# Norms and FFN of a finished half spread over 13 and 9 steps, slot scores as one stacked float32r pass, its set-up moved into the first attention

## The reference

```python
x = x + attn_a(layernorm(x))        # 16 heads of 128, causal softmax attention
x = x + ffn(layernorm(x))           # int8 quantised rows @ int8 weight, scaled, + bias, as float16
x = x + attn_b(layernorm(x))        # 16 heads, rope, 64 slots per head, gated
x = x + ffn(layernorm(x))

# ffn: q = round(x / scale), scale = max|x| per row / 127; out = (q @ w.T) * scale * w_scale + bias
# attn_b, the slot scores and what hangs on them:
s   = clip(hs @ Ws1.T @ Ws2.T + bs2, -32, 32)     # Ws1: 256 -> 16, Ws2: 16 -> 16 heads * 64 slots
z   = cumlogsumexp(s, over time); es = exp(s); enz = exp(-z)
A   = tril(rope(q) @ rope(k).T * scale)
qv  = softmax(enz * (A @ es)); W2 = tril((qv * enz) @ es.T); o = W2 @ v
out = (rmsnorm(o) * g_w * silu(g)) @ Wo.T
```

## The kernel before

| r | what |
|---|---|
| 1 | `sum_rows` (PE), `add_rows`, `ln_stats` (DVE) |
| 2 | `ln_rsqrt` (POOL), `ln_scale`, `ffn_quant` (DVE) |
| 3 | `ffn_transpose` (PE), `ffn_copy` (ACT) |
| 4 | `ffn_product` (PE), `ffn_out` (DVE), `ffn_add` (POOL) |
| 5 | `ffn_add`, `ln_rsqrt` (POOL), `ln_stats` (DVE) |
| 6, 7 | `ln_scale`, `tail` (DVE), `transpose_x` (PE), `transposed` (ACT) |
| 8 | `s1_product` (PE), `s1_copy` (ACT) |

## Time and profile before

### The profile page before, as it was taken

How to read it: one execution, slowest core, us unless ns; L and a number is a source line. 1 busy time by engine, 2 the same in 40 slices (tenths; PEclk the granted TensorE clock), 3 DMA queues, 4 the chain that set the end, 5 groups by cost and what they waited for, 6 DMA issues and landing times.

```text
span 836.5 us, 13230 instructions
## 1 busy us (share of the span) xinstructions
PE 775.7 (93%) x4550; PEld 658.7 (79%) x4550; DVE 595.8 (71%) x1510; ACT 475.2 (57%) x1261; POOL 375.0 (45%) x356
## 2 busy tenths in 40 slices
PE   7999999998989998977897999999996999999973
PEld 6878888887878886866776888888885878888862
DVE  5545555567764457878797888888887788888855
ACT  4656656655565665644545666665663556666520
POOL 5243223223332243552645656665572665666411
PEclk9999999999999999988999999999999999999997
DMA  8211111121111221110101101111210111110100
GB/s 258 78 51 51 62 53 51 56 84 44 50 50 59 78 63 39 39 50 13 52 13 51 50 28 56 58 42 35 63 52 13 52 39 39 62 53 13 38 1 25
DMA packets 43283, 43.22 MB, mean 52 GB/s; under 512 B 3521, under 2 KB 42945, under 8 KB 43090
## 3 DMA queue, kind: packets, MB, share of 16 engines
q1 hardware_dynamic: 43218, 42.38, 16.0%
HBM read 41.33 MB, written 1.05 MB: 51 GB/s over the span
## 4 chain that ended last, share of the span: by engine, by line
PE 80%; DVE 11%; ACT 4%; issue 2%; POOL 2%; DMA 1%; SPq 0%; POOLq 0%; DVEq 0%; ACTq 0%
PE ps L1454 19%; PE ps L1643 10%; PE ps L1530 6%; PE ps L1461 5%; PE ps L1487 4%; PE ps L1657 3%; PE ps L1535 3%; PE ps L1512 3%; PE ps L1495 2%; PE ps L1684 2%; PE ps L1704 2%; PE ps L1723 2%; PE ps L1705 2%; PE ps L1670 2%; PE ps L1658 2%
## 5 line engine op out<-in xcount | busy, mean ns | idle before, releaser
L403 POOL TENSOR_TENSOR w_lo<-w_raw,w_hi 128x512 fp32r<-128x512 f32 x64 | 82.0, 1293 | 85.4 <-ACT w_hi L599 84.5
L1454 PE MATMUL ps<-xT_hi,w_hi 128*128 128x512 f32 x256 | 110.0, 430 | 4.2 <-ACT rot_s L747 2.3
L1149 DVE TENSOR_TENSOR wt<-ps,const 128x384 f32<-128x384 f32 x128 | 68.1, 553 | 47.2 <-PE ps L1658 27.3
L1454 PE MATMUL ps<-xT_hi,w_lo 128*128 128x512 f32 x256 | 101.4, 396 | 0.0
L1454 PE MATMUL ps<-xT_lo,w_hi 128*128 128x512 f32 x256 | 101.2, 395 | 0.0
L471 POOL TENSOR_TENSOR rot_s<-rot_s,const 128x512 f32<-128x512 f32 x64 | 81.4, 1282 | 20.4 <-ACT rot_s L747 20.4
L659 ACT ACTIVATE wt<-wt,negmax 128x128 f32<-128x128 f32 (+1 forms) x128 | 56.7, 444 | 21.9 <-DVE negmax L1044 21.8
L403 POOL TENSOR_TENSOR wc_lo<-wv,wc_hi 128x512 fp32r<-128x512 f32 x16 | 20.4, 1274 | 100.1 <-ACT wc_hi L599 100.1
L1032 DVE TENSOR_TENSOR v<-ps,bv_b 128x256 f32<-128x256 f32 x64 | 26.9, 422 | 50.7 <-PE ps L1461 50.7
L493 POOL TENSOR_TENSOR qp<-oke,enz 128x256 f32<-128x256 f32 x32 | 23.7, 739 | 83.4 <-ACT oke L771 83.4
L1137 DVE RECIPROCAL enz<-zs 128x128 f32<-128x128 f32 x64 | 60.3, 942 | 0.0
(11 more groups left out here) (159 smaller groups left out, 2354.6 us busy)
## 6 DMA issues: line engine op xcount, KB each, us to landing
w_raw<-a_w_q SPq DMA_DIRECT2D x16, 256.0 KB, 3.1
w_raw<-a_w_k SPq DMA_DIRECT2D x16, 256.0 KB, 3.8
...
```

Source lines behind the costliest of these rows:

```text
L403: g.tensor_tensor(lo[:, :, :], raw[:, :, :], hi[:, :, :].bitcast(F32), ALU.subtract).then_inc(ph.w_lo, 1)
L1149: d.tensor_tensor(dst, src[:, 0:384], tri3, ALU.mult).then_inc(done, 1)
L1454: ins = mm(PJ[bank], w[:, m, c, h * P:(h + 1) * P], x[:, c, cols], start=(t == 0), stop=(t == len(terms) - 1))
```

## The change

The extra work of a half is now written once, as `portion(f, half, r)` with `f` = 0 for the FFN between the attentions and `f` = 1 for closing, and fills `r` = 1 to 13 (`f` = 0) or 1 to 9 (`f` = 1):

| r | PE | DVE | ACT | POOL |
|---|---|---|---|---|
| 1 | `sum_rows` x2 | `add_rows` x2 | | |
| 2 | | `ln_stats` x2 | | |
| 3 | | | | `norm_half`: scale, 4 tiles of `xn` |
| 4 | | `ffn_range`, 4 tiles in one reduce | | |
| 5 | | | | `clear_sums` (`f` = 0) |
| 6 | | `ffn_round` x2 | | |
| 7 | `ffn_transpose` x2 | | `ffn_copy` x2 | |
| 8, 9 | `ffn_product` | | `ffn_scaled` | `ffn_tail` |
| 10 | | `ln_stats` x2 | | |
| 11 | | | | `norm_half` |
| 12, 13 | `transpose_x` | | `transposed` | `x_tail` |
| 13 | `s1_product` x2 | `s1_tail` x2 | `s1_copy` x2 | |

Rows 10 to 13 are for `f` = 0 alone. The tail of the program keeps its old form. Normalising, the two last operations of the FFN's output and `xT_lo` have gone from DVE to POOL, the scaling by the row scale from DVE to ACT.

The slot scores: `ws1` now has 96 columns with `Ws1` three times (at 0, 32 and 64), `ws2` three copies of `Ws2` and two of the bias, and ACT and DVE leave in `s1` the high part in rows 0 to 63 and the low part in rows 64 to 95. One float32r matmul over all 128 rows then gives hi*hi + hi*lo + lo*hi. The loads and zeroing for this stand in steps 0 to 8 of attention a and no longer at the start. The sums `accT` are cleared in step 1 and no longer in step 2. In even b steps ACT copies the turned slot weights (`slot_copy`) ahead of task "c3", and DVE clips ahead of the gate.

```diff
-        ws1 = sb("ws1", [P, C, RANK])
-        s1 = sb("s1", [P, B * T])
-        ws2 = sb("ws2", [P, HEADS * M])
+        ws1 = sb("ws1", [P, C, STACK])
+        s1 = sb("s1", [P, B * T], F32R)
+        ws2_s = sb("ws2_s", [P, HEADS * M], F32R)
+        one_rows = sb("one_rows", [P, 1])
         rot = sb("rot", [P, 2, HALF])
+        ws2 = rot[:, :, :].rearrange("p k t -> p (k t)")
...
# SP, in the loop over phases of attention a
+                if phase == 3:
+                    sp.wait_ge(init_done, 4)
+                    for o in (0, 32, 64):
+                        sp.dma_start(ws1[:, :, o:o + RANK], b_ws1.rearrange("(c p) n -> p c n", p=P)).then_inc(slot_ld, 16)
+                        sp.dma_start(ws2[o:o + RANK, :], b_ws2).then_inc(slot_ld, 16)
...
# POOL
+            def norm_half(k, half):
+
+                n, four = norms[k], slice(4 * half, 4 * half + 4)
+                pool.wait_ge(n.mv, 4 * half + 4)
+                g.tensor_scalar(var8[:, four], mv[:, four, 1], LN_EPS, None, ALU.add).then_inc(n.eps, 1)
+                pool.wait_ge(n.eps, half + 1)
+                g.tensor_tensor(rstd[:, four], var8[:, four], minus_half[:, four], ALU.pow).then_inc(n.rstd, 1)
+                pool.wait_ge(n.rstd, half + 1)
+                for t in range(4 * half, 4 * half + 4):
+                    g.tensor_scalar(xn[:, t, :], acc[:, t, :], mv[:, t, 0:1], rstd[:, t:t + 1],
+                                    ALU.subtract, ALU.mult).then_inc(n.xn, 1)
+
+            def ffn_tail(f, b):
+
+                F, two = ffns[f], slice(2 * (b % 2), 2 * (b % 2) + 2)
+                pool.wait_ge(F.y, b + 1)
+                g.tensor_tensor(y32[:, :, :], y32[:, :, :], ws_b[:, :].unsqueeze(1).to_broadcast([P, 2, D]), ALU.mult).then_inc(F.yw, 1)
+                pool.wait_ge(F.yw, b + 1)
...
+                g.tensor_tensor(y16[:, two, :], y32[:, :, :], fb_b[:, :].unsqueeze(1).to_broadcast([P, 2, D]), ALU.add).then_inc(F.y16, 1)
+                ffn_add(f, b)
+
+            def x_tail(b):
+
+                cols = slice(b * T, (b + 1) * T)
+                pool.wait_ge(xts[1].hi, b + 1)
+                g.tensor_tensor(xT_lo[:, :, cols], xT[:, :, cols], xT_hi[:, :, cols].bitcast(F32), ALU.subtract).then_inc(xts[1].lo, 1)
...
-                if x == 2:
+                if x == 1:
                     clear_sums(None, 0)
                     clear_sums(None, 1)
...
# POOL, b_step: even and odd steps
                         rope_mul(ahead, "q1", 0, 1)
+                    portion(0, 1, x)
+                    portion(1, 0, x - PHASES)
                     if nxt:
                         slots(x + 1)
...
                         rope_mul(ahead, "k1", 1, 1)
+                    portion(0, 1, x)
+                    portion(1, 0, x - PHASES)
                     rms(x)
...
# ACT
-                s.activation(s1[0:RANK, b * T:(b + 1) * T], ps[0:RANK, 7, o:o + T], ACT.Copy).then_inc(s1_done, 1)
+                s.activation(s1[0:STACK, b * T:(b + 1) * T], ps[0:STACK, 7, o:o + T], ACT.Identity,
+                             bias=one_rows[0:STACK, 0:1]).then_inc(s1_hi, 1)
+            def ffn_scaled(f, b):
...
+                for t in range(2):
+                    ins = s.activation(y32[:, t, :], ps[:, 7, t * D:(t + 1) * D], ACT.Copy, scale=qsc[:, 2 * b + t:2 * b + t + 1])
+                ins.then_inc(F.y, 1)
...
                 if x % 2 == 0:
+                    slot_copy(x)
                     b_task(phase, "c3")
-                    slot_copy(x)
...
# DVE
+            def s1_tail(b):
+
+                cols, o = slice(b * T, (b + 1) * T), (b % 2) * T
+                dve.wait_ge(s1_hi, 2 * (b // 2) + 2)
+                d.tensor_tensor(s1[64:STACK, cols], ps[64:STACK, 7, o:o + T], s1[64:STACK, cols].bitcast(F32),
+                                ALU.subtract).then_inc(s1_done, 1)
...
                 if x % 2 == 0:
+                    if rest:
+                        b_clip_s(ahead)
                     b_gate(phase, 3)
-                    if rest:
-                        b_clip_s(ahead)
-                    middle(1, x, 0)
-                    closing(r, 0)
                     b_w2_masks(x)
...
                     b_recip(phase, 3)
+                    portion(0, 1, x, 2)
+                    portion(1, 0, r, 2)
...
# PE
-                    ins = mm(ps[0:RANK, 7, o:o + T], ws1[:, c, :], xT[:, c, b * T:(b + 1) * T],
+                    ins = mm(ps[0:STACK, 7, o:o + T], ws1[:, c, :], xT[:, c, b * T:(b + 1) * T],
...
+            def portion_done(f, half, r):
...
                 if r == 7:
-                    pe.wait_ge(xts[1].lo, b + 2)
+                    pe.wait_ge(F.qT, b + 2)
                 if r == 8:
+                    pe.wait_ge(F.y, b + 1)
+                if r == 9:
+                    pe.wait_ge(F.y, b + 2)
+                if r == 12 and f == 0:
+                    pe.wait_ge(xts[1].hi, b + 1)
+                if r == 13 and f == 0:
                     pe.wait_ge(s1_done, b + 2)
...
                         ins = mm(PJ[bank][:, t * P:(t + 1) * P], s1[:, tile * P:(tile + 1) * P],
-                                 ws2[:, pair * P:(pair + 1) * P], start=True, stop=True)
+                                 ws2_s[:, pair * P:(pair + 1) * P], start=True, stop=True)
```

More of the change, by code:

```diff
@@ L453, in _ @@
+                if r == 9:
+                    ffn_tail(f, b + 1)
+                if f == 0:
+                    if r == 11:
+                        norm_half(2, half)
+                    if r == 12:
+                        x_tail(b)
+                    if r == 13:
+                        x_tail(b + 1)
             pool.wait_ge(init_done, 1)
@@ L535, in a_step @@
                                     ).then_inc(bo_done, 1)
-                middle(0, x - PHASES)
+                portion(0, 0, x - PHASES)
             def b_step(x):
@@ L811, in b_step @@
                         b_task(ahead, "s")
-                        middle(1, x)
-                        closing(x - PHASES)
+                        portion(0, 1, x, 0)
+                        portion(1, 0, x - PHASES, 0)
                         b_task(ahead, "q0")
@@ L856, in _ @@
             s.activation(sums[:, :], const[:, K_TRI:K_TRI + 2 * P], ACT.Copy).then_inc(b_sums, 1)
-            for x in range(1, LAST - 1):
+            for x in range(1, 8):
+                a_step(x)
+            act.wait_ge(ones_done, 1)
+            act.wait_ge(slot_ld, 16 * 8)
+            s.activation(ws2_s[:, :], ws2[:, :], ACT.Copy).then_inc(ws2_hi, 1)
+            for x in range(8, LAST - 1):
                 a_step(x)
@@ L1212, in b_step @@
                         b_scores(x + 1)
-                    middle(1, x, 1)
-                    closing(r, 1)
                     b_gated(x)
@@ L1236, in b_step @@
                         b_rope_add(ahead, "k0")
-                    middle(1, x, 0)
-                    closing(r, 0)
+                    portion(0, 1, x, 0)
+                    portion(1, 0, r, 0)
                     b_w2_masks(x)
@@ L1247, in b_step @@
                         ln_scale(3, 2)
-                        ffn_quant(1, 2)
+                        ffn_quant(2)
                     if nxt:
                         b_scores(x + 1)
-                    middle(1, x, 1)
-                    closing(r, 1)
+                    portion(0, 1, x, 1)
+                    portion(1, 0, r, 1)
                     if rest:
@@ L1268, in b_step @@
                         b_slots(x + 1)
-                middle(1, x, 2)
-                closing(r, 2)
             for x in range(LAST - 1):
@@ L1558, in a_step @@
                 a_task(ahead, o)
-                middle(0, r, 0)
+                portion(0, 0, r, 0)
                 a_turn(x, 1)
@@ L1562, in a_step @@
                 a_scores(x + 1)
-                middle(0, r, 1)
+                portion(0, 0, r, 1)
                 a_values(x)
```

319 lines of the change are left out of this document (133 added, 186 removed).

## The result

| | before | after |
|---|---|---|
| median of the timed runs, us (runs) | 844.62 (4) | 815.12 (4) |
| lowest and highest | 842.74, 844.79 | 813.33, 816.53 |
| profiled execution, its span | 838.3, 836.5 | 816.11, 814.0 |
| busy PE, DVE, ACT, POOL (before: see its profile) | | 768.4, 581.7, 481.2, 423.2 |
| ratio to before (95% interval) | | 0.9654 (0.9628 to 0.9681) |

29.5 us less; the forecast was 39.3 less, 805.4. The windows of after, with the columns of rows 1: the start that was 10.86, eight undisturbed steps of a, half 0 with step 30, half 1, two undisturbed steps of b, closing.

The account below looks back on a forecast made before the run. PE bounds undisturbed steps; beside the FFN halves it stalls 49.8 us on late DVE. 49.8 - 17.0 returned + 4.6 slot scores + 1.9 start = 39.3 less: 844.7 to 805.4 us, forecast's own range 798 to 813, overall 790 to 820.

Parts of the forecast that it names:

- step 6 and 22: DVE's rounding beside POOL's lo parts overflows its gap and may be held: 0.3 to 3.5 us back, taken 1.8, twice.
- step 8 and 24: Three POOL operations of some 3.7 us in a 3.45 gap ahead of `qp`, DVE held: 0.3 to 3, taken 2.0.
- step 9 and 25: The same 3.7 us on POOL in the 3.43 ahead of the rms norm: 0.3 to 2, taken 0.7, twice.
- step 12: Two more ACT copies ahead of the squares, and `x_tail` on POOL: 0 to 2 us back, taken 0.7, once.
- `s1`, step 13: In half 1 PE's last group waits for `s1_tail`, which stands behind `s1_copy` and the output copy: 1.5 us back.
- half 0: Returns beside attention a: 2.6 us for PE's wait on `s1_tail`, 2.0 for POOL beside DVE's weight scaling; 4.6 together.
- scaling, steps 3, 11, 19: Four tiles scaled on POOL, at most 4.3 us in a 3.43 gap: 0 to 2 back, taken 0.4 three times.
- all that returns: Stall time coming back in half 0 (4.6), half 1 (7.5) and closing (4.9): 17.0 us, ends about 5.5 and 32.
- slot scores: Four one-pass float32r products per phase in place of float32: 4.6 us gained, bounds 0 and 7.
- start: DVE's wait for the clearing of `accT` in step 2 of attention a goes: 1.9 us gained.
- POOL holds DVE deeply: Rival: returns at their upper end of 32, PE at 1.2 GHz in some steps; 820 us, chance 0.14.
- Narrow float32r is no faster: Rival: 128-column float32r products in the slot scores run no faster than float32; 810 us, chance 0.14.

Follow-up runs that it names:

- slot_f32: Changed kernel with the four slot-score products of each phase reading the same stacked tiles as plain float32; 815.57 us, ratio 0.9681.
- norm_two: Changed kernel with POOL scaling two tiles in steps 3 and 11, two in 4 and 12, and the range moved to step 5; 814.23 us, ratio 0.9671.
- norm_dve: Changed kernel with the scaling of all five half-norms on DVE, behind the output tail of steps 3 and 11; 814.57 us, ratio 0.967.
- norm_dve_idle: Changed kernel with the scaling of half 1 and closing on DVE where it idles, ahead of the odd step's last gate; 805.75 us, ratio 0.9569.
- tail_last: Changed kernel with POOL's three FFN-tail instructions behind the slot weights and k0 product of steps 8 and 24; 811.12 us, ratio 0.963.

## Why the prediction was right, and where not

The direction and the range held, and the mechanism is the one forecast: the stalls of before go, and a part returns through POOL. The terms, in the forecast's order; a step's excess is its length over the undisturbed one, less its own new work, as in the prediction:

| term | forecast | measured (trace) |
|---|---|---|
| step 6 and 22 | 1.8 each | 1.4 each |
| step 8 and 24 | 2.0 each | 2.15 each (16.62 - 14.02 - 0.45) |
| step 9 and 25 | 0.7 each | 0.5 each (14.01 - 13.05 - 0.44) |
| step 12 | 0.7 | 0.3 (14.74 - 14.02 - 0.44) |
| `s1`, step 13 | 1.5 | 1.5, with a wait of 1.31 |
| half 0 (against the same steps of before) | 4.6, of it `s1` 2.6 | 5.3: 3.6 in step 29, with a wait of 2.64 for `s1`; 1.8 in step 30 |
| scaling, steps 3, 11, 19 | 0.4 each | 4.5, 5.6, 5.6 |
| all that returns | 17.0 | 30.9 |
| slot scores | -4.6 | -3.8 in steps (8 x 0.33 + 7 x 0.17), 0 in time (slot_f32) |
| start | -1.9 | -2.0 (8.82 for 10.86) |
| tail, to the end of the span | 0 | +2.2 (43.86 for 41.62) |

**The step that failed** is "Steps 3 and 11: four tiles scaled on POOL ... 0 to 2, taken 0.4". I bounded a tile from above by 0.74, a two-input operation on as many elements; it took 1.24. The piece was 6.34 and not 4.3 at most, and it was 2.9 late where 0.9 had been the worst. That the scaling did it is shown: with it cut in two (norm_two) or moved off POOL (norm_dve, norm_dve_idle) these steps fell to 13.5, 13.1 and 15.0. A second omission made it larger: I priced the lateness and not the half clock behind it, which in after came with the waits of 2.69 (0.90, 0.82) and not with those of 1.31 and 2.07 (1.00). The other terms of what returns sum to 15.2 against 15.8, though not each for its reason: the 2.0 for holds in half 0 did not show, and 1.8 came in step 30, where PE's wait for `rot_s`, 2.34 in before, was 2.82 and the clock 0.89. The ends of the returns, given as 5.5 and 32, add up by the list to 5.9 and 34.3.

**The median was carried over wrongly.** By the terms above the span should shrink by 49.8 - 30.9 + 3.8 + 2.0 - 2.2 = 22.5, and it did (836.5 - 814.0); the profiled execution's own time fell by 22.2. The timed gain is 7.3 more. The difference between before's profile and its median, which I carried over whole, was by all signs half clock in its stalls: 0.976 there and 0.966 to 0.970 in most of the executions of before that were timed beside the variants, an estimated 0.007 x 840 = 6, and with the stalls most of it went (after: 0.976 to 0.978 in all four). So an error of 14 one way met one of 7 the other way, and that the range held is luck: with the trace's gain alone the median would have been 844.6 - 22.2 = 822.4, outside it.

**Of the rivals**, "POOL holds DVE deeply" had the number nearer (820), for returns at their upper end; but the holds were as forecast (the rope sum of step 8 took 1.78, 1.15 over its 0.63, within the bound of 1.6), and what went past its upper end was POOL's own lateness. The Trainium skill (GPSIMD Engine Reference, "Engine selection") calls one-input operations roughly line-rate on GpSimd. Measured here, the scaling of 256 elements is 1.24 us on POOL and 1.37 / 4 = 0.34 on an undisturbed DVE, and the measurement decides. "Narrow float32r is no faster" is wrong in the records, four with starts 0.11 to 0.14 apart where before had eight, and right in the time.

**The signs that I named**: the wait for `qb` down to the tail's, the four records, a pair of steps at 27.06 to 27.25 (forecast 27.1), waits for `s1` of 2.64 and 1.31 (2.6 and 1.5) and the rope sum over 1 us in step 8 all came. Idle PE of 12 did not (20.6 without step 30), nor a clock of 0.99 or 1 (0.98), nor a long rope sum in step 12. PE waited for `qp` in two steps of these and never long for the masks, so the condition that I named for being wrong was not met; it named the wrong tile.

**Not settled:** why the tail is longer. Its last step took 27.2 in both traces of before and 28.3 to 30.0 in after and all variants. Its three long waits are the same in after to 0.04; the clock was 0.82 and is 0.75, which by length times missing clock is an estimated 4.9 and 7.5, nearly all of the difference. Why the clock is lower there, no run tells. Open too are how much of tail_last's 4.0 us is its own, the clock in slot_f32, and why every other even step is 0.17 longer. And no run spreads the work over more steps without moving it to POOL and ACT, so the share of each in the 49.8 is not known.
